# Two conditioned attention layers on one core: layer 1's query product split into row halves, with a PSUM bank for even and one for odd heads

## What is computed

```
q = softmax(q.reshape(b, t, h, dh), axis=-1)      # over a head's 64 features
k = softmax(k.reshape(b, t, h, dh), axis=1)       # over the tokens
v = ((xn @ Wv + bv) * src_mask).reshape(b, t, h, dh)
att = einsum('bnhd,bnhl->bhdl', k, v)             # a 64 x 64 block per head
y = einsum('bnhd,bhdl->bnhl', q, att)
hh = silu(_ln(y) * (1 + scale) + shift) @ W_out + b_out
return x + hh
```

## Time and profile before

| | |
|---|---|
| median of 3 runs | 1055.71 us (1054.01 to 1057.61) |
| the profiled execution | 1053.85 us, span of its instructions 1052.1 us |
| granted TensorE clock, mean | 0.998 of 2.4 GHz |
| busy TensorE matmul / weight load | 1023.2 us (97%) / 890.6 us (85%) |
| busy VectorE / ScalarE / GpSimd | 771.9 us (73%) / 611.0 us (58%) / 590.4 us (56%) |
| layer 1's attention half, L1494 | first record at 604.3 us, last at 1032.7 us |

### The profile page before, as it was taken

How to read it: one execution, slowest core, us unless ns; L and a number is a source line. 1 busy time by engine, 2 the same in 40 slices (tenths; PEclk the granted TensorE clock), 3 DMA queues, 4 the chain that set the end, 5 groups by cost and what they waited for, 6 DMA issues and landing times. The chain is left out here.

```text
span 1052.1 us, 26045 instructions
## 1 busy us (share of the span) xinstructions
PE 1023.2 (97%) x8558; PEld 890.6 (85%) x8558; DVE 771.9 (73%) x1346; ACT 611.0 (58%) x2021; POOL 590.4 (56%) x872
## 2 busy tenths in 40 slices
PE   7999999999999999999998899999999999999997
PEld 6679888898889888898886778888888888888885
DVE  7656766678666876667677787878778877778885
ACT  6358766776768767687677454434444444443353
POOL 4455456554566555654577466665556555566632
PEclk9999999999999999999999999999999999999999
DMA  9652111220112111121122211222211111111101
GB/s 319 227 184 66 45 45 52 55 65 32 55 42 65 55 32 59 48 65 47 43 79 86 81 56 56 66 67 65 65 65 48 47 55 60 56 58 65 45 31 51
DMA packets 46118, 73.74 MB, mean 70 GB/s; under 512 B 8274, under 2 KB 14546, under 8 KB 46068
## 3 DMA queue, kind: packets, MB, share of 16 engines
q1 hardware_dynamic: 46066, 73.11, 21.7%
q10 hardware_dynamic: 2, 0.00, 0.0%
HBM read 56.28 MB, written 16.81 MB: 69 GB/s over the span
## 5 line engine op out<-in xcount | busy, mean ns | idle before, releaser
L670 ACT ACTIVATE prob<-prob,neg_max 128x128 f32<-128x128 f32 x512 | 198.6, 395 | 78.2 <-DVE neg_max L973 78.2
L1335 PE MATMUL bank<-xt_hi,w_hi 128*128 128x256 f32 x752 | 213.9, 284 | 0.0
L483 POOL TENSOR_SCALAR stat<-stat 128x1 f32<-128x1 f32 x128 | 34.4, 269 | 318.0 <-DVE stat L935 298.0
L1336 PE MATMUL bank<-xt_lo,w_hi 128*128 128x256 f32 x752 | 209.5, 279 | 0.0
L1337 PE MATMUL bank<-xt_hi,w_lo 128*128 128x256 f32 x752 | 209.4, 279 | 0.0
L1335 PE MATMUL bank<-w_hi,xt_hi 128*128 128x512 f32 x384 | 157.5, 410 | 0.3 <-DVE w_lo L896 0.3
L1337 PE MATMUL bank<-w_hi,xt_lo 128*128 128x512 f32 x384 | 151.3, 394 | 0.0
L1336 PE MATMUL bank<-w_lo,xt_hi 128*128 128x512 f32 x384 | 150.4, 392 | 0.0
L1335 PEld LDWEIGHTS bank<-xt_hi,w_hi 128*128 128x128 f32 x752 | 141.7, 188 | 1.4 <-DVE z_a L1008 0.2
L1336 PEld LDWEIGHTS bank<-xt_lo,w_hi 128*128 128x128 f32 x752 | 141.7, 188 | 1.3
L1337 PEld LDWEIGHTS bank<-xt_hi,w_lo 128*128 128x128 f32 x752 | 141.8, 189 | 0.0
(11 more groups left out here) (129 smaller groups left out, 2347.3 us busy)
## 6 DMA issues: line engine op xcount, KB each, us to landing
x_in<-in_x_dram SPq DMA_DIRECT2D x32, 256.0 KB, 2.8
x_res<-in_x_dram SPq DMA_DIRECT2D x32, 256.0 KB, 2.6
between_layers<-x_res SPq DMA_DIRECT2D x32, 256.0 KB, 2.0
x_in<-between_layers SPq DMA_DIRECT2D x32, 256.0 KB, 3.3
x_res<-between_layers SPq DMA_DIRECT2D x28, 256.0 KB, 2.6
out_dram<-x_res SPq DMA_DIRECT2D x28, 256.0 KB, 2.0
room<-in_L_cond_W_emb_dram SPq DMA_DIRECT2D x8, 512.0 KB, 6.6
prob<-in_L_cond_emb_w_dram SPq DMA_DIRECT2D x4, 512.0 KB, 10.9
```

The source lines that it names most:

```text
L483: pool.tensor_scalar(v[:, 8:9], v[:, 7:8], EPS, None, ALU.add).then_inc(s[a_in].sem, 1)
L670: last = act.activation(prob[:, b, i, :], prob[:, b, i, :], ACT.Exp, bias=neg_max[:, b, i:i + 1], accum_out=row_sum[:, b, h:h + 1])
L1335: pe.matmul(o, a_hi, b_hi, start=start, stop=False)
L1336: pe.matmul(o, a_hi, b_lo, start=False, stop=False)
```

## The change

1. `query` makes eight matmuls in place of four. Each takes 64 rows of `q_feat` (one head's features; all 128 token columns stay stationary) and that head's 64x64 block (64 moving columns). Even heads use the upper half of the array's rows and one bank, odd heads the lower half and another bank.
2. `Y` in the tables now names two banks for each sequence; `H` in `DRAIN` moves from (0, 3) to (6, 7). `query` claims both banks.
3. `y_norm` in layer 1 makes two instructions, one for each bank: 128x256 in, written to alternate 64-column blocks of `y_s`.
4. The memset of `kv_blocks`, its two waits on POOL and VectorE's wait for it are gone, since the zero quarters are no longer read.

```diff
-        SECOND = dict(X=(0, 1), K=(6, 7), V=(0, 6), Q=(2, 4), KT=(2, 4), QT=(3, 3), KV=(4, 4), Y=(5, 1), H=(3, 7), O=(5, 1))
+        SECOND = dict(X=(0, 1), K=(6, 7), V=(0, 6), Q=(2, 4), KT=(2, 4), QT=(3, 3), KV=(4, 4), Y=((5, 2), (1, 7)), H=(3, 7), O=(5, 1))
-        DRAIN = SECOND | dict(V=(0, 3), Q=(2, 4), KT=(6, 7), QT=(2, 4), KV=(0, 3), Y=(6, 7), H=(0, 3), O=(5, 4))
+        DRAIN = SECOND | dict(V=(0, 3), Q=(2, 4), KT=(6, 7), QT=(2, 4), KV=(0, 3), Y=((6, 7), (0, 3)), H=(6, 7), O=(5, 4))
...
-                if i == G - 1:
-
-                    for g in range(2):
-                        pool.wait_ge(*done(s[f"pt_pe{g}"], LAST0))
-                    pool.memset(per_seq[:, 2 * GROUP:3 * GROUP, :], 0.0).then_inc(zeroed, 1)
...
+                    for h in range(2):
+                        last = dve.tensor_tensor(
+                            to[:].rearrange("p (c h e) -> p h c e", c=C, h=2)[:, h],
+                            bank[bk["Y"][b][h]][:, 0:C * DH1].rearrange("p (c e) -> p c e", c=C),
+                            q_rec[:, kslot, b, :].rearrange("p (c h) -> p h c", h=2)[:, h:h + 1, :]
+                            .rearrange("p h c -> p c h").broadcast_to([P, C, DH1]), ALU.mult)
+                last.then_inc(s["y_norm"].sem, 1)
...
-                    dve.wait_ge(zeroed, 1)
...
             def query(k, b, bk=SECOND):
                 to = bk["Y"][b]
-                claim(to, (s["y_norm"], k + b))
+                for h in range(2):
+                    claim(to[h], (s["y_norm"], k + b))
                 pe.wait_ge(*done(s["att_out"], k + b))
                 pe.wait_ge(*done(s["qt_out"], k + b))
                 for c in range(C):
-                    last = pe.matmul(bank[to][:, c * P:(c + 1) * P], q_feat[b][:, c * P:(c + 1) * P],
-                                     kv_blocks[b][:, c * P:(c + 1) * P], start=True, stop=True)
+                    for h in range(2):
+                        rows = slice(DH1 * h, DH1 * (h + 1))
+                        last = pe.matmul(bank[to[h]][:, c * DH1:(c + 1) * DH1], q_feat[b][rows, c * P:(c + 1) * P],
+                                         kv_blocks[b][rows, c * P + DH1 * h:c * P + DH1 * (h + 1)],
+                                         start=True, stop=True, tile_position=(DH1 * h, 0))
                 last.then_inc(s["y_pe"].sem, 1)
```

More of the change, by code:

```diff
@@ L213, in build @@
         w_split = [[sem(f"w_split{l}{j}") for j in range(4)] for l in range(2)]
-        zeroed = sem("zeroed")
         def stages(names, first=0):
@@ L993, in y_norm @@
                     dve.wait_ge(*done(s["rec"], k + b))
-                    yb, h, rc = bank[FIRST["Y"][b]], H0, rec0[:, b, :]
+                    hv = lambda ap: ap.rearrange("p (h e) -> p h e", h=H0)
+                    last = dve.tensor_tensor(hv(to[:]), hv(bank[FIRST["Y"][b]][:]),
+                                             rec0[:, b, :].rearrange("p (h o) -> p h o", o=1).broadcast_to([P, H0, DH0]),
+                                             ALU.mult)
                 else:
                     dve.wait_ge(*done(s["qrec"], k + b))
[L997 to L1001, removed]
+                    for h in range(2):
[5 more added lines that the diff above has]
+                last.then_inc(s["y_norm"].sem, 1)
                 dve.wait_ge(*done(s["y_norm"], k + b))
```

## The result

The change made the kernel slower: 1062.76 us in the median of 8 runs (1060.58 to 1065.2), against 1055.25 of 8 runs of the kernel before (1053.21 to 1058.81). The ratio is 1.0062, 95% interval 1.0045 to 1.0079: slower by 0.6%. The forecast was 1062.0. The profiled execution took 1064.8 us, its span 1063.0.

The account below looks back on a forecast made before the run. TensorE bounds the kernel, matmuls busy for 97% of the span. Query 0 +2.3, query 1 +3.8 and drain +0.2 sum to +6.3 us on 1053.85, 1060.2; the runs' median lies 1.9 higher, so 1062.0, range 1058 to 1067.

Parts of the forecast that it names:

- The load sets the round, 0.11 as before: In query on TensorE: halving the moving columns leaves eight rounds at 0.11 us each, 1.04 us a call.
- A change of tiling costs 0.09 ahead and 0.09 behind, and 0.11 more for the load that is not hidden: Around query on TensorE: query 0 +0.15, query 1 +0.33 in the 8 calls without a late kv_out.
- Late steps: a stall of 0.01, so +0.17: At query 1 in 7 of 15 calls: 1.71 us against 1.54, the load due at 0.34 against a possible 0.33.
- 7 of 15 calls at 1.54: Query 1 in the kernel before: 7 calls start their load late, 1.54 us each; the other 8 take 1.38.
- `y_norm` +0.18: On VectorE in layer 1: two 128x256 instructions take +0.18 us a call over the whole one's 0.68.
- Drain +0.2: In the drain, y_norm's extra +0.18 lies on VectorE's chain once: +0.2 us.
- Memset and banks 0: The dropped memset (0.95 us) hides in POOL's 5.39 us wait for z_a; second banks bring no new wait: 0.
- What the profile would show: A step 0.4 us longer, no extra wait behind kv_out; wrong if kv_out ends more than 0.1 late.
- (b): In query, load and move of a tile do not overlap: 0.16 a round, 11 over 30 calls, 1073; chance 0.05.
- (c): VectorE's chain takes over, y_norm's halves at their upper bound: +6.4 and 0.5 in the drain, 1069; chance 0.05.
- (d): Lost elsewhere: steps shift, a late kv_out disappears, a wait's gain eats half the cost: +2, 1058; chance 0.08.
- (a): In query the move sets the round: 0.62 a call; 1051.6, or 1054.5 if y_norm's halves cost 0.18; chance 0.06.

Follow-up runs that it names:

- half_load: The change with only 64 of the 128 token columns loaded and an empty instruction behind query's waits; one run, 1054.5 us, a call 0.61.
- wide_move: The change with 128 moving columns for each matmul instead of 64, memset kept; one run, 1064.84 us, a call 1.09.
- change_kv_first: The change with kv_out ahead of y_norm on VectorE, in step1 and drain; 1062.76 us, ratio 1.0051 to the kernel before.
- before_kv_first: The kernel before with kv_out ahead of y_norm on VectorE, in step1 and drain; 1057.98 us, ratio 1.0006 to the kernel before.
- halves_only: The kernel before with layer 1's y_norm in two instructions and the old query; 1057.95 us, ratio 1.0012 to the kernel before.
- tiles_only: The change with y_norm left as one instruction that reads the even heads' bank for all heads; 1062.03 us, ratio 1.0057 to the kernel before.
- memset_kept: The change with the memset of kv_blocks and its waits put back; one run, 1061.25 us, first query to the end 454.0.
- four_tiles: The change with query's matmuls also split by tokens, four 64x64 tiles, and an empty instruction behind the waits; 1055.30 us, ratio 0.9989 to the kernel before.
- four_tiles_kv_first: The change with query in four 64x64 tiles, an empty instruction behind its waits, and kv_out ahead of y_norm in step1; 1051.26 us, ratio 0.9957 to the kernel before.

## Why the prediction was right, point by point

- *The load sets the round, 0.11 as before.* Right, by half_load and wide_move: 1.04 for a call, forecast 1.04.
- *A change of tiling costs 0.09 ahead and 0.09 behind, and 0.11 more for the load that is not hidden.* Right: query 0 +0.15, early query 1 +0.33; with no stall at all, +0.49 a step (change_kv_first against before_kv_first). The Trainium skill, "TensorEngine Tiling (Array Packing)", section "Key Properties", says that changing the tiling mode drains TensorE; 0.21 against 0.12 in front of query 0 fits that and would be its price here, but no record shows the drain itself.
- *Late steps: a stall of 0.01, so +0.17.* This was mis-sized, and here the mechanism was short. The forecast had `kv_out` 0.27 after the last projection record (measured 0.19 to 0.28, in the mean 0.23) and then let the load follow within 0.07, as in the earlier trace rows. It follows by 0.22, because of the wait instruction that the second bank brings. The forecast had looked at the banks for lateness alone and put them at nothing. Six late steps cost +0.35 each instead of +0.17: +1.1 us.
- *7 of 15 calls at 1.54.* The count was right and the length was not. One of the seven is the first step's, at 2.12, and two are 1.44 and 1.45; the six of the twelve steps have a mean of 1.51. The other calls are 1.37 in the mean, against 1.38.
- *`y_norm` +0.18.* Mis-sized: 0.76 for the two halves against 0.69, +0.07. The row that gave 0.88 is of another instruction (SCALAR_TENSOR_TENSOR). With +0.18 the late steps would have been worse still.
- *The rest of a step.* The forecast took it as unchanged. Before had the shorter distance of the 256-column records in 10 of 12 steps, the change in 4: +0.5 us over the twelve.
- *Drain +0.2.* Wrong in sign: -0.9. VectorE L1067 and the normalising instruction on GpSimd, before and then after:

```profile
1027.63 1.17 DVE L1067 TENSOR_TENSOR room<-spare,q_max 128x512 f32<-128x512 f32 x1
...
1035.83 1.31 POOL L518 TENSOR_SCALAR yn<-y_s,stat 128x512 f32<-128x512 f32 x1 [0.21 <-POOL stat L486]
```
```profile
1039.42 0.83 DVE L1067 TENSOR_TENSOR room<-spare,q_max 128x512 f32<-128x512 f32 x1
...
1044.11 0.75 DVE L996 TENSOR_TENSOR y_s<-bank,q_rec 128x256 f32<-128x256 f32 x2
...
1047.34 0.77 POOL L517 TENSOR_SCALAR yn<-y_s,stat 128x512 f32<-128x512 f32 x1 [0.21 <-POOL stat L485]
```

  L1067 is 0.34 shorter and the GpSimd instruction 0.54. `y_norm` starts 1.37 after the start of the last pair of `query` calls instead of 1.80, and `turn_yn` comes 4.15 behind it (at 1048.26) instead of 4.62: that is the 0.9. The runs part the two. The GpSimd instruction takes 0.77 in every kernel with `y_norm` in halves, halves_only among them, and 1.31 in the three without (before, before_kv_first, tiles_only). L1067 is short with the new `query` (0.77 in tiles_only) and stays long with the halves alone (1.22 in halves_only). Why either is shorter is not shown.
- *Memset and banks 0.* Right for the memset, by memset_kept. For the banks it was wrong in late steps: no reader of a second bank was late, but the wait for it is an instruction, and it costs 0.15 where it stands behind a late `kv_out`.

- *What the profile would show.* A step is 0.53 longer and not 0.4, the load behind `kv_out` has an extra wait, and the stall of up to 0.22 is past the 0.1 that was named as a sign of being wrong.

The sum came out right partly by luck. The twelve steps' +6.4 are query 0 12 x 0.15 = 1.8, early query 1 6 x 0.33 = 2.0, late query 1 6 x 0.35 = 2.1 and the distance of the records 0.5. Against the forecast of +6.3 in all, the late steps and the record distance gave 1.6 more, the drain 1.1 less, and the first step, counted at +0.3, lengthened by nothing.

Of the rivals, (b) and (c) did not happen. (d) had the right place, an exchange between waits and shifts, but its items went both ways. (a) was refuted as a theory of this kernel, since the load and not the move sets the round; but its 0.62 a call is what four tiles take (0.63). (Its early load is due at 0.15 + 0.28 = 0.43, not 0.41.) Both of its times, 1051.6 and 1054.5, have `kv_out` come no sooner, and the kernel of that kind, four_tiles, took 1055.30. That four_tiles_kv_first took 1051.26 is near the first of them by chance, as it has `kv_out` first.

## What to carry to other kernels

Look at what sets a round before halving anything: two tiles with 64 moving and 128 stationary columns take as long as one matmul with all rows, and splitting the stationary columns too is what makes the call short. Add a change of tiling on both sides (0.09 each here) and the load behind it that nothing hides (0.11). A second bank also means one wait more, and a wait instruction behind the one that ends last costs its 0.11 to 0.15 even if it is long fulfilled: look in the trace which wait stands last. And where the shorter call then waits for another engine, the list of that engine has to be put in order first, or the gain stays in the wait: a step of 29.09 us against 28.70, a ratio of 0.9989 against 0.9957.

## What was not expected of the hardware

- A weight load starts 0.07 us after the end of the VectorE instruction that it waits for when that wait is in the last wait instruction, and 0.18 or 0.22 after it when a fulfilled one stands behind. In all three cases the load starts 0.03 behind the end of the last wait instruction, with tiles or without. How the waits are packed changed with an empty instruction put in; what decides it stays open.
- 256-column projection records stand 114.1 or 116.1 ns apart, the same through a step, and which it is changed with edits that touch neither. Open.
- Stretches at 1.2 GHz of 3.4 or 6.8 us, at the start and at the change of layers, differ between kernels whose code is nearly the same up to there. The first `query` comes between 604.4 and 611.7 over all kernels here. One trace has such a stretch in the drain, behind a wait of TensorE of 2.03 us.
- A VectorE instruction of 128x512 between SBUF tensors took 0.77 to 1.62 us and one of GpSimd 0.77 or 1.31 in the same place of the drain. Edits to the work beside them moved both; that they stretch each other is argued, not shown.
